# Two convolution-attention blocks on one Trainium2 core: in the second block's first half, queries as one product of 512 columns, a merged mask, attention one step sooner

## What is computed

```python
x = x + L0(_gn(x))        # block 0: q, k, v by 1x1 and depthwise 3x3; softmax attention, silu, projection, norm
x = x + L1(_gn(x))        # block 1, with _gn over 32 groups of 4 channels per image:
    qkv = einsum('bchw,oc->bohw', x, w_qkv)              # 384 channels
    y = grouped 1x1 of 8 (depthwise 5x5 (qkv))           # 384 channels more
    mqkv = concatenate([qkv, y])                         # 32 heads: 16 from qkv, 16 from y
    q, k = relu(mqkv[:, :, :8]), relu(mqkv[:, :, 8:16])  # v is the rest, with a row of ones added
    vk = einsum('bhdn,bhen->bhde', v, k)
    out = einsum('bhde,bhen->bhdn', vk, q)
    out = out[:, :, :-1] / (out[:, :, -1:] + 1e-15)
    x = bn(einsum('bchw,oc->bohw', out, w_proj))        # folded into one projection and a bias
```

## Time and profile before

| | |
|---|---|
| time, median of 3 runs | 326.14 us (325.75 to 330.5) |
| profiled execution | 326.22 us, span from first to last instruction 324.5 us |
| TensorE busy | 262.7 us (81%), mean granted clock 0.963 |
| VectorE busy | 204.5 us (63%) |
| ScalarE busy | 150.9 us (46%) |
| GpSimd busy | 122.7 us (38%) |
| instructions | 13486 |

### The profile page before, as it was taken

The page is one execution under the profiler, slowest core; times in us unless marked ns, Lnnn a source line. Parts: engine busy times, 40 slices in busy tenths (PEclk is TensorE's granted clock), DMA queues, the critical chain, the costliest instruction groups (busy, mean ns, idle before and its releaser), DMA issues. The chain is left out here.

```text
span 324.5 us, 13486 instructions
## 1 busy us (share of the span) xinstructions
PE 262.7 (81%) x5763; PEld 199.7 (62%) x5763; DVE 204.5 (63%) x696; ACT 150.9 (46%) x372; POOL 122.7 (38%) x311
## 2 busy tenths in 40 slices
PE   0348799569799789966959999979898899879995
PEld 0235676348586676755647677757677777667771
DVE  3798886219996267998796766562323323458774
ACT  0456674148962568673563355330432336822220
POOL 8144664008695447744330232110223322133300
PEclk9999999859999799998799999997999999999999
DMA  7730099941002400000017082633100000001112
GB/s 232 118 81 10 18 199 204 219 121 29 4 6 47 79 3 4 2 0 1 2 40 159 19 182 56 145 75 91 36 4 4 4 4 4 5 2 51 66 50 97
DMA packets 15883, 20.07 MB, mean 62 GB/s; under 512 B 4288, under 2 KB 9408, under 8 KB 15808
## 3 DMA queue, kind: packets, MB, share of 16 engines
q1 hardware_dynamic: 12256, 18.03, 23.8%
q10 hardware_dynamic: 3568, 1.18, 2.1%
HBM read 4.33 MB, written 2.30 MB: 20 GB/s over the span
## 5 line engine op out<-in xcount | busy, mean ns | idle before, releaser
L1074 PE MATMUL bank<-cin,tband 64*32 64x240 f32 (+2 forms) x3072 | 87.8, 377 | 14.5 <-DMA cin<-cin 7.5
L1074 PEld LDWEIGHTS bank<-cin,tband 64*32 64x32 f32 x3072 | 68.7, 109 | 32.6 <-issue 13.2
L891 DVE STREAM_TRANSPOSE cpos<-bank 128x256 f32<-128x256 f32 x96 | 36.4, 423 | 52.3 <-PE bank L1074 52.1
L573 ACT ACTIVATE tband<-tband,row_edge 128x96 f32<-128x96 f32 (+1 forms) x96 | 32.4, 397 | 40.4 <-POOL tband L409 38.9
L1070 PE MATMUL bank<-ident,rings 128*128 128x128 f32 x192 | 33.0, 301 | 17.0 <-ACT rings L512 8.1
L1070 PEld LDWEIGHTS bank<-ident,rings 128*128 128x128 f32 x192 | 22.4, 150 | 29.1 <-ACT rings L512 10.7
L843 DVE STREAM_TRANSPOSE cin<-bank 128x768 f32<-128x768 f32 x32 | 30.9, 976 | 14.8 <-PE bank L1074 14.8
L445 POOL TENSOR_SCALAR ring_v<-cpos,mask_b 128x512 f32<-128x512 f32 x30 | 20.9, 708 | 35.5 <-PE bank L1074 22.4
L409 POOL TENSOR_TENSOR tband<-taps,pw 128x320 f32<-128x320 f32 x24 | 17.7, 737 | 42.6 <-PE bank L1074 42.6
L512 ACT ACTIVATE rings<-bank,ln_b,ln_s 128x128 f32<-128x128 f32 x64 | 24.2, 466 | 12.8 <-POOL ln_b L397 12.8
L445 POOL TENSOR_SCALAR ring_v<-rings,mask_b 128x512 f32<-128x512 f32 x16 | 10.9, 694 | 43.1 <-ACT rings L651 43.1
(11 more groups left out here) (131 smaller groups left out, 454.8 us busy)
## 6 DMA issues: line engine op xcount, KB each, us to landing
cin<-cin SPq DMA_DIRECT2D x48, 192.0 KB, 4.3
cin<-cin SPq DMA_DIRECT2D x40, 64.0 KB, 2.0
xin<-in_x_dram SPq DMA_DIRECT2D x4, 512.0 KB, 6.3
out_dram<-rings SPq DMA_DIRECT2D x16, 128.0 KB, 1.8
taps<-tap_rows SPq DMA_DIRECT2D x16, 60.0 KB
taps<-tap_rows SPq DMA_DIRECT2D x16, 36.0 KB
cin<-cin ACTq DMA_DIRECT2D x8, 64.0 KB
rings<-in_L_conv_w_qkv_dram ACTq DMA_DIRECT2D x1, 192.0 KB, 6.7
```

The lines of the kernel that those rows point to most:

```text
L573: last = a.activation(dst[:, :, 2 + e], dst[:, :, e], ACT.Copy, scale=row_edge[:, e:e + 1])
L891: last = v.transpose(cpos[n % NS // TS][:, :, :, g * CG:(g + 1) * CG], bank[2 * (n % 4) + q][:, 0:B * HH])
L1074: return t_.matmul(dst, stationary, moving, start=start, stop=stop, skip_group_check=True)
```

## The change

Constants: the list of the steps at which convolution sets start becomes a count (`SETS_AHEAD`), the second GroupNorm chunk is closed at step 10 and not 11, and `KV_AT` is the column of bank 6 at which keys by values now lie for pairs 0 to 7 (`kv_sums`; bank 4 as before for the second half). The queries of a pair are one product of 512 columns into bank 4 (`raw_q`), emptied by one ScalarE instruction (`raw_q_out`) with semaphores `s_qp` and `s_q1`; the query parts of `qkv1` and `front1` go. `kv_mask` masks both images in two instructions, `attn_div` adds its constant in one. `attend1` and `attn_div` of pair n run at step n+1 and `o_transpose` at step n+3. `kv_product` waits in addition for the division of the pair before.

```diff
@@ -61,4 +61,5 @@
 X_BANKS = 0, 1, 3
-CONV1_STEPS = 8, 9
-GN1 = ((0, 2, 8), (2, 5, 11), (5, 8, 13))
+SETS_AHEAD = 2
+GN1 = ((0, 2, 8), (2, 5, 10), (5, 8, 13))
+KV_AT = 320
 TSLOTS = 4
@@ -230,2 +231,3 @@
         s_vr = sem("b_v_half_out_of_psum")
+        s_qp = sem("b_q_product_done")
         s_v1 = sem("b_v_ready")
@@ -281,2 +283,7 @@
             return slice(HC * n, HC * (n + 1))
+        def kv_sums(n):
+            t = bank[6][:, KV_AT:KV_AT + 2 * (QC + 1)] if n < PAIRS else bank[4][:, 0:2 * (QC + 1)]
+            return t.rearrange("p (b c) -> p b c", b=2)
@@ -631,2 +638,4 @@
                 act.wait_ge(s_kt, PAIRS) if i < 2 else act.wait_ge(s_qkv, 2 * (PAIRS + i - 1))
+                if i >= 2:
+                    act.wait_ge(s_qp, i - 1)
                 for b in range(2):
@@ -641,3 +650,2 @@
                 act.wait_ge(s_o, PAIRS) if i < 2 else act.wait_ge(s_v1, i - 1)
-                act.wait_ge(s_pr, PAIRS) if i < 2 else act.wait_ge(s_num, i - 1)
                 for n in range(2):
@@ -649,5 +657,10 @@
                     a.copy(ring_b[:, i % 2, at].rearrange("p (l c) -> p l c", l=XL),
-                           ps[:, :, 2 * HC:3 * HC])
-                    a.activation(ring_d[:, i % 2, :].rearrange("p (b u m) -> p b u m", b=2, u=8)[:, :, XL * n:XL * (n + 1)],
-                                 ps[:, :, UC:US].rearrange("p u (m b) -> p b u m", b=2), ACT.Relu).then_inc(s_vr, 1)
+                           ps[:, :, 2 * HC:3 * HC]).then_inc(s_vr, 1)
+            def raw_q_out(i):
+                act.wait_ge(s_qp, i + 1)
+                act.wait_ge(s_pr, PAIRS) if i < 2 else act.wait_ge(s_num, i - 1)
+                a.activation(ring_d[:, i % 2, :].rearrange("p (b n y) -> p b n y", b=2, y=HH),
+                             bank[4][:, :].rearrange("p (n y b) -> p b n y", b=2, y=HH), ACT.Relu).then_inc(s_q1, 1)
@@ -683,2 +696,3 @@
                     front1(n)
+                    raw_q_out(n)
                 if n == PAIRS - 1:
@@ -963,10 +977,9 @@
                 dve.wait_ge(s_o, PAIRS) if n < 2 else dve.wait_ge(s_num, n - 1)
-                for b in range(2):
-                    kv = bank[4][:, b * (QC + 1):(b + 1) * (QC + 1)]
-                    v.tensor_tensor(by_quarter(ctxm[:, n % 2, b, 0:C]), over_quarters(kv[:, 0:QC]),
-                                    by_quarter(mask8[:, :]), ALU.mult)
-                    last = v.tensor_scalar(ctxm[:, n % 2, b, C:C + NH1],
-                                           mask8[:, :].rearrange("p (h d) -> p h d", d=HD1)[:, :, 0],
-                                           kv[:, QC:QC + 1], None, ALU.mult)
-                last.then_inc(s_kvm, 1)
+                kv, size = kv_sums(n), [P, 2, NQ, QC]
+                v.tensor_tensor(ctxm[:, n % 2, :, 0:C].rearrange("p b (h e) -> p b h e", h=NQ),
+                                kv[:, :, 0:QC].unsqueeze(2).broadcast_to(size),
+                                by_quarter(mask8[:, :]).unsqueeze(1).broadcast_to(size), ALU.mult)
+                v.tensor_tensor(ctxm[:, n % 2, :, C:C + NH1],
+                                mask8[:, :].rearrange("p (h d) -> p h d", d=HD1)[:, :, 0].unsqueeze(1).broadcast_to([P, 2, NH1]),
+                                kv[:, :, QC:QC + 1].broadcast_to([P, 2, NH1]), ALU.mult).then_inc(s_kvm, 1)
@@ -979,5 +992,4 @@
                 tiles = [bank[5 + b][:, 0:2 * (C + NH1)].rearrange("p (j c) -> p j c", j=2) for b in range(2)]
-                for b in range(2):
-                    last = v.tensor_scalar(den[:, s, b, :, :], tiles[b][:, :, C:C + NH1], ATT_EPS, None, ALU.add)
-                link(last)
+                sums = banks[:, 5:7, 0:2 * (C + NH1)].rearrange("p b (j c) -> p b j c", j=2)[:, :, :, C:C + NH1]
+                link(v.tensor_scalar(den[:, s], sums, ATT_EPS, None, ALU.add))
                 dv = den[:, s, :, :, :].rearrange("p b j h -> p (b j h)")
@@ -991,3 +1003,3 @@
-            for step in range(FRONT1 + PAIRS + 2):
+            for step in range(FRONT1 + PAIRS + 1):
                 work = []
@@ -997,3 +1009,3 @@
                 begun = 0
-                for c, (i0, i1, at) in enumerate(GN1):
+                for c, (i0, i1, at) in enumerate(GN1[:2]):
                     if step == at + 1 + (c == 0):
@@ -1016,5 +1028,3 @@
                     k_max(step)
-                if 0 <= n - 2 < PAIRS:
-                    attn_div(n - 2)
-                for c, (i0, i1, at) in enumerate(GN1):
+                for c, (i0, i1, at) in enumerate(GN1[:2]):
                     if step == at:
@@ -1030,2 +1040,9 @@
                     kv_mask(n - 1)
+                i0, i1, at = GN1[2]
+                if step == at:
+                    gn_variance(4, 2 * i0, 2 * (i1 - i0), gn_sums[2])
+                if step == at + 1:
+                    gn_scale(4, 2 * i0, 2 * (i1 - i0), gn_sums[2])
+                if 0 <= n - 1 < PAIRS:
+                    attn_div(n - 1)
@@ -1248,7 +1265,7 @@
                         pe.wait_ge(s_vr, 2 * i - 1 + n)
-                    units(n, ring_a[:, i % 2, :], w1t, 0)
-                    for xl in (2 * n, 2 * n + 1):
-                        last = product(bank[xl].rearrange("p (u z) -> p u z", u=2)[:, :, UC:US], w1q[:, :],
-                                       tile(ring_a[:, i % 2, :], xl))
-                    last.then_inc(s_qkv, 1)
+                    units(n, ring_a[:, i % 2, :], w1t, 0).then_inc(s_qkv, 1)
+            def raw_q(i):
+                pe.wait_ge(s_q1, i) if i else pe.wait_ge(s_gn, 4)
+                product(bank[4][:, :], w1q[:, :], ring_a[:, i % 2, :]).then_inc(s_qp, 1)
@@ -1271,5 +1288,7 @@
                 if n == 0:
-                    pe.wait_ge(s_gn, 4)
+                    pe.wait_ge(s_nrm, 2 * PAIRS)
                 else:
                     pe.wait_ge(s_kvm, n)
+                if 1 <= n < PAIRS:
+                    pe.wait_ge(s_div, n)
                 if n == PAIRS:
@@ -1283,3 +1302,4 @@
                             k, values = cpos[1][:, n - PAIRS, x, quad(q)], ring_v[:, n % 2, :, x * NQ + q, :]
-                        last = product(bank[4][quad(q), 0:2 * (QC + 1)], k, values, start=x == 0,
+                        to = kv_sums(n).rearrange("p b c -> p (b c)")[quad(q)]
+                        last = product(to, k, values, start=x == 0,
                                        stop=x == (2 * XL if n < PAIRS else XL) - 1)
@@ -1290,3 +1310,3 @@
                 pe.wait_ge(s_kvm, n + 1)
-                pe.wait_ge(s_vr, 2 * (n + 1)) if n < PAIRS else pe.wait_ge(s_qc1, n - PAIRS + 1)
+                pe.wait_ge(s_q1, n + 1) if n < PAIRS else pe.wait_ge(s_qc1, n - PAIRS + 1)
                 if n == 0:
@@ -1309,11 +1329,18 @@
-            for step in range(FRONT1 + PAIRS + 4):
+            def gn_of_block1(c, k):
+                i0, i1, _ = GN1[c]
+                if k == 0:
+                    pe.wait_ge((s_ke, s_sl, s_x1)[c], PAIRS)
+                gn_mean(2 + c, k, 2 * i0, 2 * (i1 - i0), gn_sums[c])
+            for step in range(FRONT1 + PAIRS + 2):
                 n = step - FRONT1
-                for c, (i0, i1, at) in enumerate(GN1):
-                    if c and step == at + 1:
-                        gn_mean(2 + c, 1, 2 * i0, 2 * (i1 - i0), gn_sums[c])
                 if 0 <= step - 6 < PAIRS:
                     z_transpose(step - 6)
+                if step == GN1[1][2] + 1:
+                    gn_of_block1(1, 0)
                 if 0 <= step - 4 < PAIRS:
                     project(step - 4)
+                if step == GN1[1][2] + 1:
+                    gn_of_block1(1, 1)
                 if 0 <= step - 3 < PAIRS:
@@ -1326,26 +1353,30 @@
                     kq_transpose(step)
-                for c, (i0, i1, at) in enumerate(GN1):
-                    if step == at:
-                        pe.wait_ge((s_ke, s_sl, s_x1)[c], PAIRS)
-                        gn_mean(2 + c, 0, 2 * i0, 2 * (i1 - i0), gn_sums[c])
+                if step == GN1[0][2]:
+                    gn_of_block1(0, 0)
                 if step == GN1[0][2] + 1:
-                    gn_mean(2, 1, 0, 2 * GN1[0][1], gn_sums[0])
-                if 0 <= n - 4 < PAIRS:
-                    o_transpose(n - 4)
-                if 0 <= n - 2 < PAIRS:
-                    attend1(n - 2)
+                    gn_of_block1(0, 1)
                 if 0 <= n < PAIRS:
                     qkv1(n)
+                if step == GN1[2][2] + 1:
+                    gn_of_block1(2, 1)
                 if 0 <= n - 1 < PAIRS:
                     kv_product(n - 1)
-                for j, at in enumerate(CONV1_STEPS):
-                    if n == at:
-                        if j == 0:
-                            pe.wait_ge(s_vr, 2 * PAIRS)
-                        conv(NS + j, K1)
+                if 0 <= n < PAIRS:
+                    raw_q(n)
+                if step == GN1[2][2]:
+                    gn_of_block1(2, 0)
+                if PAIRS <= n < PAIRS + SETS_AHEAD:
+                    if n == PAIRS:
```

(11 more changed lines are left out.)

## The result

The changed kernel takes 316.24 us in the median (four runs, 314.74 to 317.3), beside 325.94 for the kernel before; ratio 0.9713, 95% interval 0.9663 to 0.9763. In a later session it was 315.83 beside 325.65 (0.9719, 0.9668 to 0.9771). The profiled execution is the 314.74 one, span 313.0. Forecast were 321.7 and a range from 319.2: the direction was right, the size was not, and the time fell outside the range. Medians are of all executions; ratios leave out those over 1.5% longer than the fastest of their kernel, of which the longest, 640.91 us in the later session at a granted clock of 1.00, has no known cause.

What follows compares the result with a forecast made beforehand. It took steps 4 to 7 as bound by TensorE plus a small wait for VectorE's mask. Set 16 starting 3.65 us earlier plus 0.9 in the second half gave 4.55 off 326.2: 321.7 us, range 319.2 to 324.5.

Steps and rivals of the forecast that it cites:

- Steps 0 to 3: Block 1's first steps: new waits early and in step 3, step 1's 3.36 wait gone; step 4 only 0.6 us earlier.
- The wait for the aggregates: Step 0: TensorE waits about 2.2 us for the first GroupNorm sum of pairs 2 to 4, now before the last projection.
- VectorE's third chain: Step 3: the third GroupNorm scale, 12 chained instructions behind pair 2's mask, slowed beside GpSimd to 3.76 us.
- The stall: Step 3: TensorE idles 2.35 us before the first attention-output transpose, which waits for VectorE's GroupNorm scale to finish with its bank.
- The full step: Steps 4 to 6 of block 1's first half: 6.57 us each, 0.80 less than 7.37.
- Rival C: Step 3: the clock falls in the new stall, costing 1.7 to 2 us, total 323.6; chance 0.13.
- T: End of the last `conv_in` in block 1's first half: forecast 209.6 us, 4.3 earlier than 213.9.
- Set 16 ... I keep that loss of 1.7: Convolution set 16, after the gap: still runs at half clock, so its loss of 1.7 us stays.
- rival B: TensorE keeps its full clock into set 16: 1.7 us more gained, total 320.0; chance 0.10.
- The DMAs land 0.65 later: Before set 16: ScalarE's four DMAs, issued behind the last query copy, land 0.65 us later and delay the set.
- 0 if SyncE's are the last anyway: Lower bound on the delay of set 16's DMAs: none if SyncE's transfers land last; upper bound 0.95 us.
- The second half: Second half's loop: merged mask at its head gains 0.8 us and denominators 0.07, together 0.9 (bounds 0.3 and 1.0).

Runs made afterwards that it cites:

- the one without the stall: Changed kernel, first output transpose waiting only until the GroupNorm sums are copied out of bank 7, not for the whole VectorE chain: 311.64 us, ratio 0.9623.
- The split kernel: Changed kernel with the VectorE mask again as four instructions and the denominator as two: 317.68 us, ratio 0.9796.
- the filler: Kernel before, with two further 512-column products in the gap ahead of set 16: 323.07 us beside 326.11, ratio 0.9932.

## Why the prediction was wrong, by its own steps

**Steps 0 to 3: right in their waits, 1 us too long in step 0.** Taken from the LayerNorm transpose, that is with 2.09 added to the times after, step 1 starts at 162.3 (forecast 163.4), step 2 at 168.6 (170.1), step 3 at 175.8 (176.7). The wait for the aggregates is 2.16 (2.2), and VectorE's third chain runs from 178.36 to 181.98, 3.6 long (3.76), with three instructions of 0.46 to 0.66 where the others take 0.17. The stall is 2.25 (2.35). The early steps are about 1 sooner. The clock isn't the reason: step 0 takes 6.57 or 6.58 in all seven profiles of the changed kernel and its variants with the wide product, at granted clocks from 0.76 to 0.88. The changed kernel, then the one without the stall:

```profile
153.66:160.24 6.58, 5.38 (x72) 3.20 (x72) 6.16 (x28) 2.10 (x7) 1.70 (x9) 0.83 0.01 2
153.58:160.15 6.57, 5.83 (x71) 3.36 (x71) 6.16 (x28) 2.07 (x7) 1.69 (x9) 0.76 0.00 0
```

VectorE is busy for 6.16 of it, and step 1 waits for ScalarE's copy behind the `conv_in`, 1.20 here and 0.74 in the second row's profile: VectorE sets the pace. From `qkv1(0)` to the first `conv_in` its work took 4.71 (153.66 to 158.37), where the forecast had 5.4 (156.1 to 161.5). That term was mis-sized.

**The full step: mis-sized.** "New step: 1.44 + 1.44 + 1.06 + 0.87 + 0.58 + 1.18 = 6.57" is 2.73 + 1.06 + 0.96 + 0.44 + 1.07 = 6.26. Each term was read from a step in which it stood beside other neighbours. The wide product itself was 0.09 dearer; but two units back to back, transposes behind the wide product and attention behind them were 0.40 cheaper together. The earlier trace rows had the product at that shape, and no row of before had this sequence.

**Rival C came true**, at its price: step 4 took 7.95, 1.7 over a clean one. So T came only 0.5 sooner than forecast (209.1 on the forecast's scale against 209.6), though a clean step was 0.3 shorter and step 4 started 1.1 sooner: over three steps the forecast is 2.0 too late by these and 1.7 too early by C, which nearly cancel. That T was so close is luck.

**"Set 16 ... I keep that loss of 1.7": failed.** The set ran at full clock, so 1.7 more; in its number that is rival B. The kernel before hadn't always had the loss there: in its second profile it stood in step 2. In this stage each of its two profiles shows one such loss, and so do the two of the changed kernel; I had counted it in set 16 and not in step 4, where it was now. B and C had been priced as rivals of each other; they came together and cancel. A loss that I read from one execution as belonging to one place was the error, not the mechanism of the low clock.

**"The DMAs land 0.65 later": failed.** The issues did start 1.1 later. The step that fails is that every DMA lands equally long after its issue: in the repeat of the kernel before SyncE's fourth, which the set waited for, took 3.5 and ScalarE's 2.1, in the changed kernel both took 2.1. So ScalarE's later issues cost nothing, and the set stands behind the division of pair 6 instead, 5.18 after T and not 6.44. That is 1.26 of error; even the bound of "0 if SyncE's are the last anyway" (5.79) was too high.

**The second half: right.** 1.05 against 0.9; mask 0.6 as forecast, and the wait of 0.97 is gone. The split kernel gives it back.

**The sum.** The profiled execution lies 7.0 below the forecast: 0.5 for T, 1.3 behind T, 1.7 in set 16, 0.15 in the second half, and 3.3 in stretches whose instructions didn't change (2.09 ahead of the stage, 1.24 in the convolutions). These vary: over eight profiles with the change or most of it the LayerNorm transpose starts at 148.1 to 150.9 and the convolutions take 49.1 to 52.5; over four of the kernel before or nearly so, 149.6 to 151.2 and 50.3 to 52.6. They overlap, and I take most of it as chance; that is not shown, since the means differ by 1.4 and 0.9. By the ratios the gain is 9.4 and 9.2 us in two sessions, each with an interval of about 1.6 to either side. What the profiles account for is 7.1 plus 1.05 in the second half (1.8 to 2.1 beside the two profiles of before, one of them with the filler, whose second half also has a low stretch, 0.96 granted). The rest, about 1 us, lies within the interval.

Where the 7.1 stands, by the first two profiles: -1.69 ahead of step 0, then 0.15, 4.47, 0.21, -1.35, -0.59, 1.10 and 1.11 for steps 0 to 6, 1.38 for step 7 up to T, 0.61 up to set 16 and 1.69 up to set 17. So most of it comes from step 1, where the wait of 3.36 was, and two thirds of that are lost again ahead of step 0 (the new wait of 2.16) and in step 3 (the stall). The gain of the full steps, 1.1 each, is what stays.

The range was too narrow for a reason that the text could have seen: its bounds varied single terms, but the step's neighbours, the landing and the clock's place all stood at their values of one execution, and all three moved: the step and the landing towards the shorter time, the clock's place to no effect in the sum.

## What to carry to other kernels

A TensorE record's cost depends on its neighbours: gathering eight scattered small products into one full-bank product took 0.87 us off a step, of which only 0.32 was in the product. A wait on VectorE that protects a bank should be for the instruction that last reads the bank, not for the chain behind it: that removed a 2.25 us stall and the half-clock stretch behind it, 3.45 us in all. And a low-clock stretch seen in one profile need not belong to the place where it stands: set 16 had it in one of three profiles with the same or a longer wait ahead of it, step 4 in every profile with the stall. Profile the kernel twice before its loss is kept or dropped in a sum.

## What was unexpected of the hardware

A 64 KB transfer within SBUF lands mostly in 2.0 to 2.3 us, but two or three in a row took 2.8 to 3.5, at varying places. The queries took 1.28 us start to start as eight records of 128 columns in two places, and 0.96 as two of 512; a group of four transposes took 0.73 to the next product behind 64 small ones (0.07 of it idle), and 0.44 behind the wide one. A wait of 3.36 us left the clock at 1.00 in one execution, and a wait of 3.35 at the same place was followed by 0.81 over the next step in another; one of 2.0 to 2.3 in step 3 was followed by a slow step 4 in all four profiles that had it. Step 0 took the same 6.57 us at granted clocks of 0.76 and 0.88, since VectorE set its pace.
